# An attention phase in which the value product streams the probabilities and the softmax divisors travel through memory

## What is computed

```python
xn = layernorm(x) * g_norm
q, k, v = xn @ Wq, *split(xn @ Wkv)            # q: 16 heads of 64; k, v: one head of 64
q, k = l2norm(q) * q_scale, l2norm(k) * k_scale
scores = 8 * q @ k.T + rel_pos_bias + causal_mask     # and one null score for each row and head
p = softmax([null_score, scores])
o = p[null] * v_null + p[keys] @ v                    # 16 heads of 64 side by side
h = layernorm(o @ Wout) * g_out
```

## Time and profile before

| what | value |
|---|---|
| median of 3 runs | 2561.74 us (2558.45 to 2563.37) |
| the profiled execution: its own time is its span | 2563.2 us |
| TensorE busy | 2394.0 us, 93% |
| VectorE busy | 1753.9 us, 68% |
| POOL busy | 1333.1 us, 52% |
| ScalarE busy | 1234.0 us, 48% |
| 32 value products L478 (2560 instructions) | 342.4 us busy |
| VectorE waiting for outp, in all | 89.9 us |

### The profile page before, as it was taken

One profiled execution on the slowest core, in us unless ns is written; L12 is line 12 of the kernel. 1 busy time (PEld: TensorE's weight loads), 2 busy tenths in 40 slices (PEclk: granted clock), 3 DMA queues, 4 the chain that ended last, 5 costly groups with the idle time before them and its releaser, 6 DMA issues. The chain is left out here.

```text
span 2563.2 us, 56453 instructions
## 1 busy us (share of the span) xinstructions
PE 2394.0 (93%) x20705; PEld 1977.5 (77%) x20705; DVE 1753.9 (68%) x4121; ACT 1234.0 (48%) x3133; POOL 1333.1 (52%) x1464
## 2 busy tenths in 40 slices
PE   5999999999999999977999999988899999999998
PEld 3788888888888888845777777766677877778776
DVE  4576767677767676677888888337865755746764
ACT  3656666666666666554555555114333333332332
POOL 3676767676767676535666666215422322322332
PEclk8999999999999999988999999999999999999999
DMA  4000100000000000001122221216022112111211
GB/s 143 7 11 9 46 18 11 10 10 9 11 10 9 10 5 5 5 15 24 40 56 55 55 53 47 55 59 181 32 66 63 55 58 67 58 47 62 66 34 59
DMA packets 156689, 105.05 MB, mean 41 GB/s; under 512 B 85168, under 2 KB 134832, under 8 KB 156416
## 3 DMA queue, kind: packets, MB, share of 16 engines
q1 hardware_dynamic: 130928, 62.69, 9.0%
q10 hardware_dynamic: 25488, 38.73, 4.9%
HBM read 80.51 MB, written 20.88 MB: 40 GB/s over the span
## 5 line engine op out<-in xcount | busy, mean ns | idle before, releaser
L968 POOL TENSOR_TENSOR a_bm<-a_bias,a_mask_add 128x512 f32<-128x512 f32 (+3 forms) x512 | 438.4, 873 | 189.3 <-DVE a_nm L697 186.3
L1592 POOL TENSOR_TENSOR m_hid_part<-m_hid,m_hid_part 128x512 fp32r<-128x512 f32 x176 | 238.5, 1355 | 552.9 <-ACT m_hid_part L1501 547.6
L874 ACT ACTIVATE a_S<-a_S,a_nm 128x512 f32<-128x512 f32 (+3 forms) x512 | 289.3, 565 | 347.6 <-DVE a_nm L697 344.9
L697 DVE CUSTOM_DVE_ANT_0 a_S<-a_S,a_bm,a_nsn 128x512 f32<-128x512 f32 (+3 forms) x512 | 275.3, 545 | 142.1 <-PE a_S L455 137.4
L478 PE MATMUL a_O<-a_v,a_PT 128*128 128x64 f32 x2560 | 342.4, 265 | 0.0
L478 PEld LDWEIGHTS a_O<-a_v,a_PT 128*128 128x128 f32 x2560 | 328.4, 193 | 0.0
L1513 ACT ACTIVATE m_hid<-m_G 128x512 f32<-128x512 f32 x176 | 105.4, 599 | 390.9 <-PE m_G L1447 353.3
L455 PE MATMUL a_S<-a_kT,a_qT 128*128 128x384 f32 (+3 forms) x1024 | 284.0, 358 | 3.6 <-DVE a_nm L697 3.2
L1674 DVE TENSOR_TENSOR m_hid<-m_hid,m_U 128x512 f32<-128x512 f32 x176 | 121.0, 687 | 223.8 <-PE m_U L1447 190.3
L1464 PE MATMUL m_Y<-m_hid_part,m_down_high 128*128 128x512 f32 x704 | 256.5, 405 | 12.2 <-POOL m_hid_part L1592 11.4
L1447 PE MATMUL m_G<-m_in,m_gate_high 128*128 128x512 f32 x704 | 252.2, 399 | 0.9 <-POOL m_up_low L1586 0.9
(11 more groups left out here) (323 smaller groups left out, 5348.4 us busy)
## 6 DMA issues: line engine op xcount, KB each, us to landing
m_spread<-s_w ACTq DMA_DIRECT2D x64, 256.0 KB, 3.2
m_spread<-s_w ACTq DMA_DIRECT2D x128, 128.0 KB, 2.9
a_x<-in_x SPq DMA_DIRECT2D x32, 128.0 KB, 2.2
s_hT<-a_hT SPq DMA_DIRECT2D x32, 128.0 KB, 2.1
d_x<-in_x SPq DMA_DIRECT2D x8, 512.0 KB, 4.7
d_h<-s_hT SPq DMA_DIRECT2D x8, 512.0 KB, 5.2
s_xg<-d_xg SPq DMA_DIRECT2D x8, 512.0 KB, 3.1
d_x<-s_xg SPq DMA_DIRECT2D x8, 512.0 KB, 4.6
```

The lines of the kernel that those rows point to most:

```text
L697: dve.tensor_tensor_reduce(S[:, n % S_SLOTS, 0:w], SB[n % 2][:, 0:w], bm[:, n % BM_SLOTS, 0:w], -1.0, nsn[:, tile % 2, h:h + 1], ALU.add, ...
L874: act.activation(S[:, n % S_SLOTS, 0:w], S[:, n % S_SLOTS, 0:w], ACT.Exp, scale=-1.0, bias=nm[:, tile % 2, h:h + 1], accum_out=den[:, tile ...
L968: pool.tensor_tensor(bm[:, n % BM_SLOTS, 0:w], bias[:, h, L - w:L], mask_add[b % 2][:, 0:w], ALU.add).then_inc(s["bm_ready"], 1)
L1592: pool.tensor_tensor(hid_part[1][:, q % H_SLOTS], hid[:, q % G_SLOTS], hid_part[0][:, q % H_SLOTS].bitcast(F32), ALU.subtract).then_inc(hi ...
```

## The change

In the value product the operands change roles. Before, the turned probabilities of one head (128 x 128) are loaded as weights and the 64 value columns streamed; the output has query rows as partitions. Now the values (128 x 64) are loaded and the turned probabilities streamed, two heads together, one into partitions 0 to 63 of bank O and one into 64 to 127, each in its half of the array's columns. The output then already stands turned, so `oT` and its copies fall away. What was a divisor for each row (partition) is now needed along the columns: the reciprocals (128 x 8 for half of the heads) are turned on TensorE (`wT0`, `wT1`), copied by VectorE, written to memory (4 KB) and read back by two DMAs of 64 partitions each, one row given to 64 partitions. Then `scale0` and `scale1` multiply bank O by them straight into oT. The probabilities have 4 slots in place of 3, pairs are done at every second head step, and the tables FRONT, BACK and the positions of diff0 and weigh0 change. The statistics of outp become a step of their own, `ostat`.

```diff
-    QK_LAG, PV_LAG, S_SLOTS, PT_SLOTS = 2, 4, 5, 3
+    QK_LAG, PV_LAG, S_SLOTS, PT_SLOTS = 2, 4, 5, 4
...
+        weightT = sb("weightT", [NH // 2, 2, P])
+
         o = sb("o", [P, NH, DH])
+        weight = o[:].rearrange("p (i a) d -> p i (a d)", i=2)
...
         FRONT = {"stat": -5, "xn": -3, "xT": -2, "q0": 0, "q1": 1, "kv": 2, "ss": 3, "qn": 4, "kT": 7,
-                 "null": 10, "qs0": 8, "qs1": 9, "qT0": 12, "qT1": 12, "qT2": 13, "qT3": 14}
-        BACK = {"diff1": 0, "weigh1": 4, "oT": 6, "pnT": 7, "outp": 9, "hn": 11, "hT": 13}
+                 "null": 10, "qs0": 8, "qs1": 9, "qT0": 13, "qT1": 13, "qT2": 14, "qT3": 15}
+        BACK = {"diff1": 0, "scale0": 1, "weigh1": 2, "wT1": 3, "pnT": 7, "scale1": 8, "outp": 9, "ostat": 11, "hn": 12,
+                "hT": 14}
...
-                    behind.setdefault(NH * t + 10, []).append(("diff0", t))
-                    behind.setdefault(NH * t + 13, []).append(("weigh0", t))
+                    behind.setdefault(NH * t + 8, []).append(("diff0", t))
+                    behind.setdefault(NH * t + 10, []).append(("weigh0", t))
+                    behind.setdefault(NH * t + 11, []).append(("wT0", t))
...
-                 "pnT": 1, "outp": 0, "hT": 1, "nullo": 0, "wide0": 0, "wide1": 1}
+                 "pnT": 1, "outp": 0, "hT": 1, "wT0": 1, "wT1": 0, "nullo": 0, "wide0": 0, "wide1": 1}
...
+                    elif name in ("wT0", "wT1"):
+                        i = int(name[2])
+                        n = 2 * t + 1 + i
+                        sp.wait_ge(s["weightT_ready"], n)
+                        sp.dma_start(weight_rows[i], weightT[:, i]).then_inc(weight_out, 16)
+                        sp.wait_ge(weight_out, 16 * n)
+                        if t == 0:
+                            sp.wait_ge(s["inv_cleared"], 16)
+                            sp.wait_ge(s["null_out_ready"], 1)
+                        else:
+                            sp.wait_ge(s["o_scaled"], 2 * t - 1 + i)
+                        for e in range(2):
+                            sp.dma_start(weight[e * DH:(e + 1) * DH, i].rearrange("p (a n) -> p a n", n=P),
+                                         bass.AP(tensor=weight_rows.tensor, offset=(i * NH // 2 + e) * P,
+                                                 ap=[[0, DH], [2 * P, NH // 4], [1, P]])).then_inc(weight_in[i], 16)
...
-                        if 0 <= n < NH * NT:
-                            tile, h = divmod(n, NH)
+                        if 0 <= n < NH * NT and n % 2 == 1:
+                            tile, h = divmod(n - 1, NH)
+                            wait_evac(pe, n - 1)
                             wait_evac(pe, n)
...
+                            at = h % 8 // 2 * P
                             for j in range(tile % TT + 1):
-                                last = pe.matmul(OB[h // 8][:, (h % 8) * DH:(h % 8 + 1) * DH],
-                                                 PT[:, n % PT_SLOTS, j * P:(j + 1) * P], v[tile // TT % 2][:, j],
-                                                 start=j == 0, stop=j == tile % TT)
+                                for e in range(2):
+                                    last = pe.matmul(OB[h // 8][e * DH:(e + 1) * DH, at:at + P], v[tile // TT % 2][:, j],
+                                                     PT[:, (n - 1 + e) % PT_SLOTS, j * P:(j + 1) * P],
+                                                     start=j == 0, stop=j == tile % TT, skip_group_check=True)
                             last.then_inc(s["pv_done"], 1)
...
-                    elif name == "oT":
-                        pe.wait_ge(s["o_scaled"], 2 * t + 2)
-                        for n in range(2):
-                            f = fill("oT", t, n)
-                            for j in range(4):
-                                i = 4 * n + j
-                                last = pe.transpose(f[:, j * P:(j + 1) * P],
-                                                    o[:, 2 * i:2 * i + 2].rearrange("p a d -> p (a d)"), ident[:])
-                            last.then_inc(full[n], 1)
+                    elif name in ("wT0", "wT1"):
+                        i = int(name[2])
+                        pe.wait_ge(s["rden_ready"], 2 * t + 1 + i)
+                        f = fill(name, t)
+                        pe.transpose(f[0:NH // 2, 0:P], rden[:, i], ident[:]).then_inc(full[FILLS[name]], 1)
...
                     elif name == "outp":
-                        pe.wait_ge(s["oT_act"], t + 1)
-                        pe.wait_ge(s["oT_dve"], t + 1)
+                        pe.wait_ge(s["o_scaled"], 2 * t + 2)
                         pe.wait_ge(s["pnrT_ready"], t + 1)
...
-                    dve.wait_ge(s["pv_done"], NH * t + 8 * (i + 1))
+
+                def scale(t, i):
+
+                    dve.wait_ge(weight_in[i], 32 * (t + 1))
+                    dve.wait_ge(s["pv_done"], NH // 2 * t + 4 * (i + 1))
                     if t > 0:
-
-                        dve.wait_ge(full[i], filling["oT", t - 1, i])
-                    dve.tensor_tensor(o[:, hs], OB[i][:, :].rearrange("p (h d) -> p h d", d=DH),
-                                      rden[:, i].unsqueeze(2).broadcast_to([P, 8, DH]),
+                        dve.wait_ge(full[0], filling["outp", t - 1, 0])
+                    dve.tensor_tensor(oT[:, 4 * i:4 * i + 4].rearrange("p a n -> p (a n)"), OB[i][:, :], weight[:, i],
                                       ALU.mult).then_inc(s["o_scaled"], 1)
...
+                    elif name in ("wT0", "wT1"):
+                        f = filled(name, t)
+                        dve.tensor_copy(weightT[:, int(name[2])], f[0:NH // 2, 0:P]).then_inc(s["weightT_ready"], 1)
+                    elif name in ("scale0", "scale1"):
+                        scale(t, int(name[5]))
...
-                    elif name == "outp":
+                    elif name == "ostat":
                         f = filled("outp", t)
```

More of the change, by code:

```diff
@@ L141, in mixture_inputs, with attention_phase @@
     return t
-def attention_phase(nc, a, ident, delta, mixture, hT_out, bias_rows, hT_dram, inv_dram):
-    QK_LAG, PV_LAG, S_SLOTS, PT_SLOTS = 2, 4, 5, 3
+def attention_phase(nc, a, ident, delta, mixture, hT_out, bias_rows, hT_dram, inv_dram, weight_rows):
+    QK_LAG, PV_LAG, S_SLOTS, PT_SLOTS = 2, 4, 5, 4
     BM_SLOTS, BM_LEAD = 6, 5
@@ L268, in attention_phase @@
         mask_loaded = [sem(f"mask_loaded{i}") for i in range(2)]
+        weight_out = sem("weight_out")
+        weight_in = [sem(f"weight{i}_in") for i in range(2)]
         FRONT = {"stat": -5, "xn": -3, "xT": -2, "q0": 0, "q1": 1, "kv": 2, "ss": 3, "qn": 4, "kT": 7,
-                 "null": 10, "qs0": 8, "qs1": 9, "qT0": 12, "qT1": 12, "qT2": 13, "qT3": 14}
-        BACK = {"diff1": 0, "weigh1": 4, "oT": 6, "pnT": 7, "outp": 9, "hn": 11, "hT": 13}
+                 "null": 10, "qs0": 8, "qs1": 9, "qT0": 13, "qT1": 13, "qT2": 14, "qT3": 15}
+        BACK = {"diff1": 0, "scale0": 1, "weigh1": 2, "wT1": 3, "pnT": 7, "scale1": 8, "outp": 9, "ostat": 11, "hn": 12,
+                "hT": 14}
         def order():
@@ L300, in attention_phase @@
         FILLS = {"xT": 0, "q0": 1, "q1": 0, "kv": 1, "qT0": 0, "qT1": 1, "qT2": 0, "qT3": 1, "kT": 0,
-                 "pnT": 1, "outp": 0, "hT": 1, "nullo": 0, "wide0": 0, "wide1": 1}
+                 "pnT": 1, "outp": 0, "hT": 1, "wT0": 1, "wT1": 0, "nullo": 0, "wide0": 0, "wide1": 1}
         filling, before, held = {}, {}, [[], []]
         for name, t in steps:
-            for n in ([0, 1] if name == "oT" else [FILLS[name]] if name in FILLS else []):
+            for n in [FILLS[name]] if name in FILLS else []:
                 filling[name, t, n] = len(held[n]) + 1
@@ L315, in drained @@
                     "qT2": [(s["qT_act"], 2 * t + 2)], "qT3": [(s["qT_dve"], 2 * t + 2)],
-                    "kT": [(s["kT_read"], t + 1)], "oT": [((s["oT_act"], s["oT_dve"])[n], t + 1)],
+                    "kT": [(s["kT_read"], t + 1)],
+                    "wT0": [(s["weightT_ready"], 2 * t + 1)], "wT1": [(s["weightT_ready"], 2 * t + 2)],
                     "pnT": [(s["pnrT_ready"], t + 1)], "outp": [(s["hn_ready"], t + 1)],
@@ L607, in weigh @@
                     link(dve.tensor_tensor(dent[:, i], den[:, c, hs], pn[:, i], ALU.add))
-                    link(dve.reciprocal(rden[:, i], dent[:, i]))
+                    if t > 0:
+                        dve.wait_ge(full[FILLS[f"wT{i}"]], filling[f"wT{i}", t - 1, FILLS[f"wT{i}"]])
+                    dve.reciprocal(rden[:, i], dent[:, i]).then_inc(s["rden_ready"], 1)
+                    dve.wait_ge(s["rden_ready"], n)
                     if t > 0:
@@ L704, in _ @@
                             if n >= PT_SLOTS:
-                                dve.wait_ge(s["pv_done"], n - PT_SLOTS + 1)
+                                dve.wait_ge(s["pv_done"], (n - PT_SLOTS) // 2 + 1)
                             w = width(n)
@@ L768, in _ @@
                         weigh(t, int(name[5]))
```

(19 more changed lines are left out.)

2 lines of the change are left out of this document (1 added, 1 removed).

## The result

The changed kernel takes 2751.75 us (median of 4 runs, 2744.55 to 2758.55), the kernel before beside it 2562.18 (2558.45 to 2563.37): ratio 1.074, 95% interval 1.0718 to 1.0763. That is 190 us slower. The forecast was slower by 123; 2752 lies above its range.

What follows compares the result with a forecast made beforehand. TensorE was taken to bound attention, wholly in the 4-block tile, with dependency waits growing after the change. 2563.2 + 125.6 (eight batches) - 8 (edge tiles) + 6.6 (clock) = 2687, set at 2685 us; range 2575 to 2735.

Steps and rivals of the forecast that it cites:

- TensorE's own work: Value product at 0.055 us an instruction, half the old price, and fewer output turns: TensorE loses about 85 us of work.
- A: Tile start to outp, which waits for scale1: +1.8, +1.8, +0.6, -1.6 us at 1, 2, 3, 4 blocks.
- C: Outp's end to the query turns, which wait for hn: +1.9, +2.0, +1.6 us at 1, 2, 4 blocks.
- Segment D: Query turns to the next tile, with the turns a step later: +1.8, +1.5, +1.5 us at 1, 2, 4 blocks.
- The wait at the border: Next tile's first scores wait at once for qT3's copy: 0.3 + 0.68 + 0.07 us.
- The way to xT: Chain from the query turns to xT, which waits for ScalarE's copy of qT2: 4.75 us at 2 blocks.
- The clock charge: Outp at the lower clock, 1.66 us more in half of the eight 1-block tiles: +6.6 us.
- B: Outp itself, the output projection: 3.67 us, unchanged apart from the clock term.
- The rival "Clock": Lower clock in every 1- and 2-block tile, for outp and turns around it, 3 us each: 2726 us; chance 0.12.
- The first rival: Faster: TensorE's saved work is realised, 2478 us without added waits, 2520 with half eaten; chance 0.15.
- The transfer: Divisors written to memory and read back, 5.6 to 6.5 us from step 3, hidden before scale1 with 1 to 2 us margin.

Runs made afterwards that it cites:

- old product with late turns: Kernel before with only the query turns at steps 13, 13, 14, 15 and hT at 14: 2755.2 us, ratio 1.0758.
- restoring edits: Scale1 to step 7 on the version with late divisors: 2584.5 us, 37 back; statistics to 9, hn to 11 on restored query turns: 2633.6 us, 66 back.
- the last turn at the border: Kernel before with only qT3, the last query turn, at step 15 in place of 14: 2617.4 us, ratio 1.0214.
- early turns: Changed kernel with query turns back at steps 12, 12, 13, 14 and hT at 13: 2699.6 us, ratio 1.0553.
- Six fills: Six overwritten bf16 matmuls ahead of the key's turn in 1-block tiles, added to the 2572.3 us version: 2565.7 us, ratio 1.0014.
- all positions back, scale1 early and the small turn moved: Changed kernel with turns, statistics and late divisors' positions restored, scale1 at step 7, wT0 in bank F0: 2572.3 us, ratio 1.0043.

## Why the prediction was right or wrong

**TensorE's own work: right in sum.** The value product costs what the rows of the later phase said. From the start of tile 4 to the attention's last scores, TensorE's busy time (second number), with the granted clock near the end of the row, first before, then after, then the old product with late turns:

```profile
191.48:1077.65 886.17, 834.30 (x6057) 758.97 (x6057) 629.42 (x1835) 549.25 (x1726) 623.37 (x665) 1.00 0.04 12
```

```profile
207.14:1261.45 1054.31, 847.84 (x5879) 662.27 (x5880) 614.54 (x1861) 534.11 (x1693) 623.33 (x664) 0.90 0.08 24
```

```profile
215.85:1268.84 1052.99, 918.66 (x6055) 825.43 (x6056) 618.19 (x1833) 554.40 (x1721) 622.66 (x664) 0.91 0.04 10
```

The busy time went up though work was removed; the clock hides it. The old product with late turns has the same work as before and is busy 84 us more. The trace's clock records add up to 198 us at the lower level there (the mean of 0.91 is rounded), and TensorE was busy in 169 of them; half of 169 is 84. (The Trainium skill, "TensorE: Matmul & The Clock Gate", Terms, puts the penalty at the time at the low level times one less the ratio of clocks, one half. The trace agrees for the busy part of that time; of all of it, the 84 us are 0.43.) The changed kernel has 201 us there and is busy in 167, which makes some 84 of its busy time; without them 764, 70 less than before. The forecast's 85 for 32 tiles is 74 for the 28 in this stretch.

By width it was less exact. Tiles 6 and 7 of the changed kernel (3 and 4 blocks) ran at the high level throughout:

```profile
279.07:316.50 37.43, 29.66 (x227) 23.45 (x227) 24.15 (x67) 20.57 (x61) 26.36 (x24) 1.00 0.13 36
316.50:357.07 40.57, 34.62 (x274) 27.12 (x275) 27.01 (x67) 23.65 (x61) 24.90 (x25) 1.00 0.24 66
```

Before, such tiles were busy 31.7 and 38.4 us: 2.0 and 3.7 us less, where the forecast had about 3.5 and 5.

**Segments A and C: right in kind, and near in size.** Outp waited for scale1, the query turns for hn; the 4-block tile's outp came 1.5 us sooner (forecast 1.6). C was 1.0 short in the 4-block tile. The restoring edits price the two at 37 and 66 us, made one after the other and with what the clock gave back in both.

**Segment D: the right links, under-sized.** The wait at the border, priced at 1.05 us, was 0.83 in every tile of the changed kernel, so it is not what was too small. The way to xT was: in the 2-block tiles xT came 5.4 us after the first query turns (mean of six), where the chain had 4.75, and it waited for qT2 there (50.3 us in all). Then VectorE stood for xnT, 85.1 us in place of 11.7 before. In the 1-block tiles the turns at the segment's start ran at the lower clock. By itself, in the old product, the last turn at the border costs 56 us, 1.7 a tile, without any clock; there the wait is 0.8 to 1.4 us by width, and at the border shown above VectorE has a reduction ahead of the copy, which the chain did not have.

**The clock charge: the step that failed most.** The forecast charged 6.6 us, for outp in half of the 1-block tiles, and gave a wider fall of the clock 0.12. The traces show it as a mean over all 1-block tiles (B +2.5 us each, 20 us for eight), and in two places that the forecast had none: the turns behind outp, at 1.94 us for 1.06, and the start of the next tile. There the 2-block tile's projections run at the lower level, so the keys' sum of squares starts 8.2 us from the tile's start. With early turns (2699.6 us) it starts at 6.7 as a mean of the six 2-block tiles, with no lower clock in their first 8 us; before, at 6.4. Outp then comes 1.9 us later than before, which is the forecast's 1.8. So the start at the lower level is what made A 1.3 us too small there. The rival "Clock" (2726) named the mechanism but put it at 3 us a tile in two tiles of four.

The places that can be read off are B (1.7 us a batch over its charge), the 2-block tile's A (1.3) and the 1-block tile's turns (0.9): 3.9 of the 8.6 us a batch by which the forecast was short, 31 us in eight batches. The other 4.7 us are mostly C and D. So the failed step is the clock's term, put at 6.6 us, and next to it the length of C and D.

How much of the 190 is the clock by itself stays open. The lost busy time (84 us) bounds it from above, since part of it ran beside waits. Six fills that fitted the key's wait gave 7 us in a version that had little of it left (61 us at the lower level); a run of the full change with the clock held up and no fill outlasting its wait was not made.

**Where the saved work went.** With all positions back, scale1 early and the small turn moved (2572.3), TensorE still has some 70 us less to do and the kernel is 0.43% slower. The version with six fills is level within 0.14%. Its fills included, TensorE is busy from 165 us to the last scores 813.89 us of 908 (0.90), where it was 859.86 of 912 (0.94) before: 1- and 2-block tiles are 1.2 and 1.9 us longer than before, 3- and 4-block ones 1.1 and 2.1 us shorter. The excess of the narrow tiles stands in segments A (0.6 and 0.9 us) and D (0.5 and 0.9), where the small turns, their copies and the multiplication by rows are links of the chain; that these are the cause is read from the order and not tested. The first rival was wrong not by the order alone, then: restored, the order would give it 2478 to 2520, and it gave 2566.

**The transfer: right**, hidden, with more room than forecast, since the write took 1.2 us and not 2 to 2.9. Its margin is real and small. One step later for wT1, with scale1 a step earlier, used it up.
